# A two-layer sandwich of attention blocks: two of ten value copies read in place, in a TensorE loop of two cycles

## The reference, cut to what matters

```python
for i in range(6):                       # 16 heads of 64, window of 32
    x = attn_layer(shift_tokens(x), Wqkv[i], q_scale[i], k_scale[i], Wo[i]) + x
    x = ffn_layer(shift_tokens(x), ln_g[i], ln_b[i], W1[i], b1[i], W2[i], b2[i]) + x
# local attention: the 32 queries of a window see the 64 keys of
# the window before it and of its own
sim  = einsum('bhwie,bhwje->bhwij', bq, bk2) * 8.0   # masked, softmax
out  = einsum('bhwij,bhwje->bhwie', softmax(sim), bv2)
```

## Time and profile before

| | |
|---|---|
| time, median of 3 runs | 3441.85 us (3436.19 to 3443.91) |
| the profiled execution, its own time | 3438.51 us |
| its span, first to last instruction | 3436.8 us |
| PE / PEld busy | 3273.3 us (95%) / 2798.2 us (81%) |
| DVE / ACT / POOL busy | 86% / 80% / 76% |
| mean granted TensorE clock | 0.984 |
| mean traffic of the DMA engines | 67 GB/s |

### The profile page before, as it was taken

How to read it: one execution, slowest core, us unless ns; L and a number is a source line. 1 busy time by engine, 2 the same in 40 slices (tenths; PEclk the granted TensorE clock), 3 DMA queues, 4 the chain that set the end, 5 groups by cost and what they waited for, 6 DMA issues and landing times. The chain is left out here.

```text
span 3436.8 us, 161363 instructions
## 1 busy us (share of the span) xinstructions
PE 3273.3 (95%) x66105; PEld 2798.2 (81%) x66106; DVE 2964.5 (86%) x5351; ACT 2734.5 (80%) x4522; POOL 2616.0 (76%) x3358
## 2 busy tenths in 40 slices
PE   7999679999999999999999999999999999999994
PEld 5767458888888888888888888888888888888883
DVE  7777578999999999989999999999999999999974
ACT  4777458888888888888888888888888888888872
POOL 5677577777887777887778787778778778778762
PEclk9999889999999999999999999999999999999997
DMA  2000013222223222232222232222232222222221
GB/s 61 4 8 8 16 51 99 74 69 66 64 77 99 73 70 65 71 94 74 73 73 62 74 92 73 73 73 61 75 92 73 73 73 68 69 66 73 73 67 59
DMA packets 161797, 228.61 MB, mean 67 GB/s; under 512 B 42264, under 2 KB 60640, under 8 KB 161504
## 3 DMA queue, kind: packets, MB, share of 16 engines
q1 hardware_dynamic: 161632, 226.85, 24.6%
HBM read 21.00 MB, written 4.19 MB: 7 GB/s over the span
## 5 line engine op out<-in xcount | busy, mean ns | idle before, releaser
L1184 POOL TENSOR_TENSOR by_cos<-by_cos,by_sin 128x1024 f32<-128x1024 f32 x384 | 913.9, 2390 | 0.0
L1190 POOL TENSOR_TENSOR by_cos<-by_cos,norms 128x1024 f32<-128x1024 f32 x384 | 729.6, 1911 | 0.0
L1560 DVE TENSOR_TENSOR by_cos<-proj,turns 128x512 f32<-128x512 f32 x768 | 523.9, 682 | 72.3 <-ACT squares L1446 67.9
L1289 PE MATMUL proj<-qkv_hi,xs_hib 128*128 128x512 f32 x1152 | 559.7, 486 | 25.7 <-DVE by_sin L1562 12.9
L1562 DVE TENSOR_TENSOR by_sin<-proj,turns 128x512 f32<-128x512 f32 x768 | 521.5, 679 | 0.0
L1446 ACT ACTIVATE squares<-proj 128x512 f32<-128x512 f32 x768 | 443.1, 592 | 42.7 <-DVE sumsb L1566 16.1
L1566 DVE TENSOR_REDUCE sumsb<-squares 128x16 f32<-128x1024 f32 x384 | 464.1, 1209 | 0.0
L1291 PE MATMUL proj<-qkv_hi,xs_lob 128*128 128x512 f32 x1152 | 458.9, 398 | 0.7 <-issue 0.7
L1290 PE MATMUL proj<-qkv_lo,xs_hib 128*128 128x512 f32 x1152 | 456.2, 396 | 0.0
L1298 PE MATMUL ring<-ident,by_cos 128*128 128x128 f32 x3072 | 405.9, 275 | 8.8 <-ACT pTb L1425 4.5
L1298 PEld LDWEIGHTS ring<-ident,by_cos 128*128 128x128 f32 x3072 | 351.5, 141 | 57.7 <-issue 9.6
(11 more groups left out here) (190 smaller groups left out, 7850.3 us busy)
## 6 DMA issues: line engine op xcount, KB each, us to landing
v_win<-vb SPq DMA_DIRECT2D x1152, 128.0 KB
v_win<-vb SPq DMA_DIRECT2D x768, 64.0 KB
in_qkv<-L_ffn_Wqkv SPq DMA_DIRECT2D x12, 768.0 KB
wo<-L_ffn_Wo SPq DMA_DIRECT2D x6, 512.0 KB, 4.1
x_tok<-L_attn_x SPq DMA_DIRECT2D x8, 256.0 KB, 4.4
residual<-x_tok SPq DMA_DIRECT2D x8, 256.0 KB, 2.0
o_x<-residual SPq DMA_DIRECT2D x1, 2048.0 KB, 8.5
out<-o_x SPq DMA_DIRECT2D x8, 256.0 KB, 2.2
```

The source lines that it names most:

```text
L1184: nc.gpsimd.tensor_tensor(both, both, by_sin[:, j, :], ALU.add).then_inc(e[f"{w_}_added"].sem, 1)
L1190: nc.gpsimd.tensor_tensor(heads, heads, inverse, ALU.mult).then_inc(e[f"{w_}_ready"].sem, 1)
L1289: nc.tensor.matmul(out, xs_hi[:, tile], qkv_hi[:, cols], start=True, stop=False)
L1560: nc.vector.tensor_tensor(of_heads(by_cos[:, t % 2, j, cols]), heads, table(0), ALU.mult)
```

## The change

Copies: for head a = 0 window 1 is no longer copied, and for a = 1 window 3 is not. In both the 64 rows wanted already lie on the right partitions of `v` (rows 0 to 63, and rows 64 to 127). Eight transfers a tile are left, 128 counts of the semaphore instead of 160. TensorE reads these two operands from `v[rows, tile, a, i, :]`.

For that the tile's place must be known in TensorE's code, so its loop gets a body of two cycles (46 iterations instead of 92), with the base of the counts taken from a register once per pair and the cycle's number in the pair, p, as a constant.

Waits: EV also waits for the value product four tiles before, since that product now reads `v`. VM waits for the scores of its own tile instead of those of the tile before.

```diff
-        **each("v"), **{f"v_moved{m}": Events(sem(f"v_moved{m}"), 160, LEAD + 1) for m in range(PER)},
+        **each("v"), **{f"v_moved{m}": Events(sem(f"v_moved{m}"), 128, LEAD + 1) for m in range(PER)},
...
-            eng.wait_ge(moved.sem, moved.at((p + t // PER) * 160 + 160, base))
+            eng.wait_ge(moved.sem, moved.at((p + t // PER) * 128 + 128, base))
...
-                    wait_tile(sp, "s_full", t - 1, when)
+                    wait_tile(sp, "s_full", t, when)
...
-                        for n in range(1, WINDOWS):
+                        for n in (2, 3 - 2 * a):
                             sp.dma_start(out[rows:rows + KEYS, n], in_[(n - 1) * WINDOW:(n + 1) * WINDOW])\
                                 .then_inc(moved, 16)
...
-                    pe.wait_ge(e[event].sem, e[event].at(k, when[0]))
+                    base, p = when
+                    pe.wait_ge(e[event].sem, e[event].at(p * e[event].per + k, base))
...
                     wait_moved(pe, t, when)
+                    tile = where(0, when[1], t)[1]
...
-                                last = nc.tensor.matmul(out[queries, at:at + DH], pT[rows, i, queries],
-                                                        v_win[rows, t % 2, n, i, :], start=True, stop=True)
+                                values = v_win[rows, t % 2, n, i, :]
+                                if n == 1 + 2 * a:
+                                    values = v[rows, tile, a, i, :]
+                                last = nc.tensor.matmul(out[queries, at:at + DH], pT[rows, i, queries], values,
+                                                        start=True, stop=True)
...
-            def cycle(base, *place):
+            def cycle(when, *place):
                 for s_, t, token, _ in steps_of("PE", *place):
-                    step(s_, t, token, (base, 0))
+                    step(s_, t, token, when)
                 next_cycle()
+
+            def in_pair(at):
+
+                return at - at % HALVES, at % HALVES
...
-                cycle(at, at)
+                cycle(in_pair(at), at)
...
-            with nc.Fori(LAG, DEPTH * STEPS - HALVES, engines=one, hint_back_edge=True) as n:
-                cycle(n)
+            with nc.Fori(LAG // HALVES, (DEPTH * STEPS - HALVES) // HALVES, engines=one, hint_back_edge=True) as pair:
+                base = pe.snap(pair * HALVES)
+                for p in range(HALVES):
+                    cycle((base, p))
             for at in range(STEPS - HALVES, STEPS + HALVES):
-                cycle((DEPTH - 1) * STEPS + at, at, 0, PER * STEPS)
+                cycle(in_pair((DEPTH - 1) * STEPS + at), at, 0, PER * STEPS)
...
                     wait_moved(act, t + 1 - TILES, when)
+                    wait_tile(act, "pv_full", t - TILES, when)
```

## The result

The changed kernel takes 3721.56 us (median of 4 runs, 3717.75 to 3723.53) against 3442.88 us for the one before: ratio 1.0805, 95% interval 1.0791 to 1.0819, so 279 us or 8% slower. The profiled execution has a span of 3718.4 us, 281.6 more than before.

A forecast was written before the change was run, and what follows sets the result against it. TensorE was taken as the bound, its steps following one another almost without gaps. The profiled 3438.5 + 233 (streaming) + 23 (jumps) - 9 (copies) = 3685.5, plus 3.3 to the median, gave 3689 us; range 3425 to 3830 us.

The forecast's parts named there:

- The signs: Queue 8 packets throughout the loop, issue waits before S and V over 200 us, TensorE about 88%, cycles 32 to 33.5 us.
- The body is streamed: TensorE's doubled loop body, 10.6 packets or 174 KB, doesn't fit and is fetched anew each iteration; chance 0.78.
- Price per cycle: Code-fetch stalls in TensorE's loop: 2.53 us for each of 92 cycles, +233 us, bounds +132 and +329.
- The back edge: TensorE's loop branch jumps to code possibly dropped: 0.5 us for each of 46 jumps, +23 us, bounds 0 and +119.
- the second rival: TensorE's granted clock also falls, to 0.89 for a third of the layers' time: +116 us, 3805 us; chance 0.04.
- the copies' term: Moved copies no longer run beside S bursts but beside V:-1: 0.1 us gained a cycle, -9 us, bounds -32 and +9.
- No stall: TensorE's longer body stays or streams unseen, leaving only the copies' gain: 3433 us, between 3410 and 3451; chance 0.16.
- Late copies: Third rival: value copies reach the value products late; at 1 us a cycle +94 us, 3536 without stalls; chance 0.02.

The follow-up runs named there:

- slot 32: Changed kernel with the first instruction of TensorE's loop placed at slot 32 of a 256-instruction code block, nothing else: 3608.69 us, ratio 1.0484 to the kernel before.
- slot 0: Changed kernel with the first instruction of TensorE's loop placed at the start of a 256-instruction code block, nothing else: 3477.29 us, ratio 1.0101 to the kernel before.
- slot 123: The changed kernel as first measured, where TensorE's loop happens to begin at that place in a 256-instruction code block: 3721.56 us, ratio 1.0805 to the kernel before.

## Why the prediction was right, point by point

The forecast was 3689 us, the time is 3721.56, 33 us or 0.9% above. The direction and the cause, code streamed in each iteration and stalls in the bursts of small matmuls, were right. The signs came: the waits of issue before S and V are 124.3 + 89.6 = 213.9 us (over 200 forecast), a cycle takes 33.5 us, TensorE's share is 90% (88% forecast). That the number lies within 1% is in part luck: its terms were off by more, in both directions. I compare them with the matmuls' time, since that adds up to the span.

- *The body is streamed.* Right: 12 packets a pair where 10 or 11 were forecast. What the trace before could only suggest is now bracketed between 1948 and 2204 instructions.
- *Price per cycle.* Forecast 2.53 us for each of 92 cycles, +233. Measured at V, S and the projection: 88.0 + 45.6 + 29.3 = 163 us, 1.8 a cycle (189 us by the loads' waits). The term was too large by 70. What I didn't see is that it is no property of the cycle but of where the borders fall: at slot 32 the whole loss was 4.8%, at slot 0 1.0%. Taking it from two straight cycles took two places for all; that they agreed (2.52 and 2.54) made it look firmer than it was.
- *The back edge.* Forecast 23 us, with bounds 0 and 119; measured 63 us (76 by the loads' waits, the 1.65 a jump above). This term was too small, by 40. The reason for choosing the low side (the hint, and the queue that runs ahead) failed: without the hint the time is the same.
- *The clock and the busy time.* The clock was the second rival at 116 us; a third of that came, 39 us, in short falls; the one shown followed a stretch with stalls. The forecast had 0 for it. PE's busy time grew by 61 in all where the forecast had -9 (the copies' term), 70 too few. Other waits shrank by about 5. So -70 + 40 + 70 - 5 = 35 us, the difference of the spans (281.6) to the sum's 247; between the medians it is 33.
- *The copies' term.* Forecast -9, with bounds -32 and +9. The wait alone is worth -10: -22 by the mechanism named (the bursts), against +15 of the longer wait for `attnb`; 3 us stay open. The two dropped copies, which I put at 0 as not on TensorE's path, are worth -14 in a loop that stays, through that same wait; this is the step that was wrong in kind. In the streamed loop the two together are worth about 40 or 3 us by its place.
- *No stall*, the first rival (0.16), is out for this body and would have been right for one of 1948 instructions. The Trainium skill ("Runtime: NRT & Kernel Launch", section "Instruction fetch mechanics") calls the cost of crossing a block's border "mostly hidden". The run at slot 0 agrees (1.0% in all), the changed kernel at slot 123 does not (8%).
- *Late copies*: nobody waited for them. In the trace after, TensorE has no wait for a transfer, and ACT's idle time before EV is 7 us over the whole span, as before. Reading in place was not run by itself; at slot 0 the whole copies' part, with it, is 3 us faster than without.

## What to carry to other kernels

Before unrolling a loop on an engine that is busy all the time, count the body's instructions and look in the trace whether the queue that brings the engine's code is silent inside the loop; if it is, a longer body can lose that, which here cost 1% to 9%, where moving the copies gave 0.8% at best. If a body must be longer, try where it begins: the same code cost 1.0%, 4.8% or 8% by where its blocks' borders fell among the bursts of small instructions. And a transfer that nobody waits for can still be moved for gain, away from the bursts of small matmuls.

## What the runs showed of the hardware that was not expected

- A burst of 128 small weight loads and matmuls takes 1.32 us alone and 1.42 to 1.56 us with copies within the on-chip memory beside it. The projections' matmuls (L1290) take 0.40 us with and without copies beside them.
- The hint for the back edge of a streamed loop changed nothing (ratio 1.0834 without, 1.0805 with; the intervals overlap).
- The granted clock fell to 0.50 21 times in the loop, 78.5 us together, once after a stretch with TensorE busy for 6.02 of 8 us, although it is busy for over 90% of the loop.
- The limit is sharp: a body of 1948 instructions was never fetched again, one of 2204 in full, 338 packets for some 38 pairs of cycles, 9 a pair, not only what it has beyond the shorter one.
